# Routed experts as a sparse computation: token rows scattered by expert through DRAM, read back transposed in groups of 384

## The reference, cut to what matters

```
x = x + tanh(g_xattn[0]) * cross_attention(layernorm(x), ctx)
x = x + tanh(g_ffn[0])   * experts(layernorm(x))
x = x + tanh(g_xattn[1]) * causal_attention(layernorm(x), ctx, x)
x = x + tanh(g_ffn[1])   * quantised_linear(layernorm(x))

experts(xt):                                   # xt: 4096 x 256
    scores = sigmoid(xt @ gate_w.T)            # 16 experts
    idx = top_k(scores + gate_b, 4)
    w = scores[idx] / sum(scores[idx]) * 2.5   # four weights of a token
    y = sum over its four experts e of w_e * (silu(xt @ gate_e) * (xt @ up_e)) @ w2_e
    return y + shared_expert(xt)               # one more expert, for every token
```

## Time and profile before

| what | value |
| --- | --- |
| median of 3 runs | 1736.63 us (1736.21 to 1738.77) |
| profiled execution, its own time | 1737.69 us |
| span from the first to the last instruction | 1735.9 us |
| TensorE busy, share of the span | 1439.8 us, 83% |
| VectorE busy | 1275.1 us, 73% |
| ScalarE busy | 636.4 us, 37% |
| GpSimd busy | 326.5 us, 19% |
| mean granted TensorE clock | 0.93 of full speed |

### The profile page before, as it was taken

One profiled execution on the slowest core, in us unless ns is written; L12 is line 12 of the kernel. 1 busy time (PEld: TensorE's weight loads), 2 busy tenths in 40 slices (PEclk: granted clock), 3 DMA queues, 4 the chain that ended last, 5 costly groups with the idle time before them and its releaser, 6 DMA issues. The chain is left out here.

```text
span 1735.9 us, 33621 instructions
## 1 busy us (share of the span) xinstructions
PE 1439.8 (83%) x10080; PEld 756.7 (44%) x10080; DVE 1275.1 (73%) x2834; ACT 636.4 (37%) x936; POOL 326.5 (19%) x340
## 2 busy tenths in 40 slices
PE   4799955999999999999997947887878788888766
PEld 2455532555555555555554522332333233232455
DVE  4999855878787777877667637887878788785475
ACT  0455531111111111111113412665656666666530
POOL 2433332112111121111002050111111111111110
PEclk7999976999999999999998965999999999899998
DMA  5011000000000000000004761111211111110002
GB/s 182 19 37 36 19 1 0 0 0 0 0 0 0 0 0 0 0 0 0 1 0 131 213 170 34 34 34 47 55 35 34 50 51 34 33 34 2 1 0 97
DMA packets 54738, 60.00 MB, mean 35 GB/s; under 512 B 6398, under 2 KB 41982, under 8 KB 54666
## 3 DMA queue, kind: packets, MB, share of 16 engines
q1 hardware_dynamic: 49466, 54.62, 11.1%
q10 hardware_dynamic: 5200, 4.33, 0.8%
HBM read 36.34 MB, written 22.28 MB: 34 GB/s over the span
## 5 line engine op out<-in xcount | busy, mean ns | idle before, releaser
L1461 DVE TENSOR_REDUCE small<-ps 128x1 f32<-128x480 f32 (+6 forms) x768 | 419.2, 596 | 99.7 <-PE ps L1513 91.4
L1439 ACT ACTIVATE region<-ps 128x1024 f32<-128x1024 f32 (+5 forms) x384 | 322.9, 880 | 229.9 <-PE ps L1570 228.2
L956 PE MATMUL ps<-region 128*128 (+1 forms) x1632 | 378.5, 382 | 8.0 <-issue 7.5
L788 ACT ACTIVATE region<-ps 128x512 f32<-128x512 f32 x136 | 81.2, 597 | 446.8 <-PE ps L960 408.8
L956 PEld LDWEIGHTS ps<-region 128*128 (+1 forms) x1632 | 158.9, 98 | 178.4 <-issue 15.9
L1586 PE MATMUL ps<-region 128*32 128x512 f32 (+5 forms) x1792 | 196.7, 512 | 28.3 <-POOL region L1411 21.6
L970 PE MATMUL ps<-region 128*128 (+1 forms) x1632 | 201.7, 273 | 19.6 <-DVE region L896 18.1
L1513 PE MATMUL ps<-region 48*128 48x480 f16 (+6 forms) x896 | 158.7, 344 | 45.6 <-DVE small L1461 44.8
L970 PEld LDWEIGHTS ps<-region 128*128 128x128 f16 x1632 | 156.7, 98 | 63.1 <-DVE region L896 19.4
L1411 POOL TENSOR_SCALAR_AFFINE_SELECT region<-region 128x512 f32<-128x512 f32 (+2 forms) x160 | 87.7, 549 | 491.5 <-ACT region L1439 491.5
L1570 PE MATMUL ps<-region 50*128 50x512 f16 (+5 forms) x896 | 133.7, 334 | 12.7 <-issue 10.5
(11 more groups left out here) (196 smaller groups left out, 1708.6 us busy)
## 6 DMA issues: line engine op xcount, KB each, us to landing
v_parts<-region SPq DMA_DIRECT2D x16, 576.0 KB, 5.8
region<-v_parts SPq DMA_DIRECT2D x16, 576.0 KB, 3.9
region<-k_parts SPq DMA_DIRECT2D x96, 68.0 KB, 2.2
region<-q_parts SPq DMA_DIRECT2D x96, 64.0 KB, 2.1
k_parts<-region SPq DMA_DIRECT2D x16, 272.0 KB, 3.3
x_sb<-in_x ACTq DMA_DIRECT2D x8, 512.0 KB, 9.4
region<-in_w13T SPq DMA_DIRECT2D x16, 256.0 KB, 2.9
q_parts<-region SPq DMA_DIRECT2D x16, 256.0 KB, 3.3
```

Of the source, the lines that this page charges most:

```text
L956: ins = nc.tensor.matmul(o, w(wt, kh, half_), xt[:, kh, cols], start=n == 0, stop=n == 5)
L1439: nc.scalar.activation(dst, src, ACT.Exp, scale=SCALE).then_inc(s_exp, 1)
L1461: nc.vector.tensor_reduce(nmp[:, qt, half, p0:p0 + np_, place], bank[:, 0:np_ * nk].rearrange("p (h k) -> p h k", h=np_), AX.X, ALU.max).t ...
```

## The change: what it does

The expert block is written anew, and the next block gets one more step.

1. **Routing and scatter.** Per chunk, the normalised rows are split into two float16 parts in SBUF (`rows`, 1,044 bytes a token: 1,024 of data, four expert numbers, and the number of the token's first home row). TensorE transposes them, the shared expert is computed on them as before, and the routing runs on four tiles in one instruction where it can (`choose`). The sigmoid comes from ScalarE's tanh. TensorE counts with triangular and all-ones matmuls which place each token has among those of its expert (`ranks`, `slots`). GpSimd then writes each token's row to the four places in a DRAM tensor `xs` that its experts own, by 16 indirect transfers of 128 rows for each chunk.
2. **Tables.** After the last chunk three short TensorE and VectorE steps make tables: which expert group g belongs to and where its rows begin. SyncE writes a fill of 384 spare rows behind each expert's last row.
3. **Groups.** 58 groups of 384 rows, a number that is fixed in the program. SyncE reads a group from DRAM by one transposing transfer into `xgT` and its tags by another transfer. TensorE makes 12 matmuls of 384 columns and 9 of 256; the weights of the expert are addressed through a register. ScalarE makes the silu and the high part, VectorE the product, the low part, the home rows (`homes`) and the copy out of PSUM. GpSimd writes the group's 384 result rows to DRAM (`ys`) by 3 indirect transfers.
4. **Combine.** In the next block, before each chunk's layer norm, GpSimd fetches the four result rows of each of its tokens (2 MB in one transfer, one buffer), and VectorE adds them to x with the token's weights by 16 instructions of 256 columns.

The core of the diff, by engine; its last two parts (`fetch`, `combine`) stand in the next block:

```diff
+GROUP = 3 * P
+GT = GROUP // P
+STRIDE = B * L + GROUP + P
+GROUPS = (B * L * TOPK + E * (GROUP - 1)) // GROUP
+ROW = D + TOPK + 1
+ROW_BUFS = 4
+G_BUFS = 4
+Y_BUFS = 3
+FILLS_AHEAD = 4
...
             @block.sync
+                for b in range(ROW_BUFS):
+                    sp.wait_ge(s_sent[b], CHUNKS // ROW_BUFS * TC * TOPK * 16)
+                sp.wait_ge(s_tabs, 3)
+                def fill_tail(e):
+                    first = sp.value_load(tail_tab[0:1, e:e + 1], min_val=e * STRIDE, max_val=e * STRIDE + B * L)
+                    sp.dma_start(xs[bass.ds(first, GROUP), :].rearrange("(p j) n -> p (j n)", j=GT),
+                                 flat(fill)).then_inc(s_tail[e], 16)
+                for e in range(FILLS_AHEAD):
+                    fill_tail(e)
+                for g in range(GROUPS):
+                    if g + FILLS_AHEAD < E:
+                        fill_tail(g + FILLS_AHEAD)
+                    if g < E:
+                        sp.wait_ge(s_tail[g], 16)
+                    b = g % G_BUFS
+                    if g >= G_BUFS:
+                        sp.wait_ge(s_ggu, g - G_BUFS + 1)
+                        sp.wait_ge(s_home, g - G_BUFS + 1)
+                    first = sp.value_load(start_tab[0:1, g:g + 1], min_val=0, max_val=E * STRIDE)
+                    sp.dma_start_transpose(xgT[:, b].rearrange("p s k n -> p (s k) n"),
+                                           xs[bass.ds(first, GROUP), 0:D].bitcast(F16)).then_inc(s_xg[b], 16)
+                    sp.dma_start(tags[:, b], xs[bass.ds(first, GROUP), D:ROW].rearrange("(j p) n -> p j n", p=P)
+                                 ).then_inc(s_xg[b], 16)
...
             @block.gpsimd
+                for c in range(CHUNKS):
+                    if c + 2 < CHUNKS:
+                        rstd_of(c + 2)
+                    b = c % ROW_BUFS
+                    pool.wait_ge(s_slot, c + 1)
+                    for j in range(TC):
+                        for r in range(TOPK):
+                            at_ = j * TOPK + r
+                            nc.gpsimd.indirect_dma_start(
+                                out=xs, out_offset=bass.IndirectOffsetOnAxis(ap=sloti[:, b, at_:at_ + 1], axis=0),
+                                in_=rows[:, b, j, :], in_offset=None).then_inc(s_sent[b], 16)
+                for g in range(GROUPS):
+                    b = g % Y_BUFS
+                    pool.wait_ge(s_home, g + 1)
+                    pool.wait_ge(s_yout, g + 1)
+                    for j in range(GT):
+                        nc.gpsimd.indirect_dma_start(
+                            out=ys, out_offset=bass.IndirectOffsetOnAxis(ap=home[:, b, j:j + 1], axis=0),
+                            in_=y_out[:, b, j, :], in_offset=None, bounds_check=B * L * TOPK - 1,
+                            oob_is_err=False).then_inc(s_back[b], 16)
...
             @block.vector
+                for c in range(CHUNKS):
+                    choose(c)
+                    if c + 2 < CHUNKS:
+                        statistics(c + 2)
+                    hidden(c)
+                    slots(c)
+                    hidden_low(c)
+                    if c + 2 < CHUNKS:
+                        normalised(c + 2)
+                    add_shared(c)
...
+                for g in range(GROUPS):
+                    if g + 2 < GROUPS:
+                        homes(g + 2)
+                    if g + 1 < GROUPS:
+                        group_hidden(g + 1)
+                    group_out(g)
...
             @block.tensor
+                for c in range(CHUNKS):
+                    shared_gate_up(c)
+                    ranks(c)
+                    if c + 1 < CHUNKS:
+                        transposes(c + 1)
+                        logits(c + 1)
+                    shared_down(c)
...
+                for g in range(GROUPS):
+                    now = ahead
+                    if g + 1 < GROUPS:
+                        ahead = expert(g + 1)
+                        group_gate_up(g + 1, ahead)
+                    group_down(g, now)
...
+                def fetch(c):
+                    pool.wait_ge(s_comb, c * TC * TOPK + 1)
+                    nc.gpsimd.dma_start(yg[:].rearrange("p t r d -> p t (r d)"),
+                                        ys[0:B * L * TOPK, :].rearrange("(c t p r) d -> p (c t) (r d)", p=P, t=TC, r=TOPK)
+                                        [:, bass.ds(c * TC, TC), :]).then_inc(s_yg, 16)
                 for h in range(2):
+                    fetch(h)
                     ln_pool(nc.gpsimd, h, s_var, s_rstd)
                 pool.wait_ge(s_wsplit, 1)
                 with pool.Fori(0, B - 1) as b:
                     context(b)
-                    ln_pool(nc.gpsimd, (b + 1) * 2, s_var, s_rstd)
-                    ln_pool(nc.gpsimd, (b + 1) * 2 + 1, s_var, s_rstd)
+                    for h in range(2):
+                        fetch((b + 1) * 2 + h)
+                        ln_pool(nc.gpsimd, (b + 1) * 2 + h, s_var, s_rstd)
...
+                def combine(c):
+                    dve.wait_ge(s_yg, (c + 1) * 16)
+                    for r in range(TOPK):
+                        for j in range(TC):
+                            n = r * TC + j
+                            if r:
+                                hold(dve, s_comb, c * TC * TOPK + 1 + n - TC + 1, s_tick)
+                            w = weights[:, bass.ds(c * TC + j, 1), r:r + 1].rearrange("p a n -> p (a n)")
+                            nc.vector.scalar_tensor_tensor(out=tile_of(c * TC + j), in0=yg[:, j, r, :], scalar=w,
+                                                           in1=tile_of(c * TC + j), op0=ALU.mult, op1=ALU.add).then_inc(s_comb, 1)
+                    hold(dve, s_comb, (c + 1) * TC * TOPK + 1, s_tick)
                 def normalise(order, b, h):
+                    combine(b * 2 + h)
                     ln_vector(nc.vector, order, b * 2 + h, 1e-5, s_var, s_rstd, s_xn, dst=xn_halves[h])
```

More of the change, by code:

```diff
@@ L941, in comb_transposed @@
[L941 to L952 removed]
+                three = ((0, 0), (1, 0), (0, 1))
@@ new lines, in transposes @@
+                def transposes(c):
+                    if c:
+                        pe.wait_ge(s_xT, 2 * c)
+                    for part in range(2):
+                        pe.wait_ge((s_hi, s_lo)[part], c + 1)
+                        for k in range(KH):
+                            for j in range(TC):
+                                ins = nc.tensor.transpose(xT_ps[part][:, k, j * P:(j + 1) * P],
+                                                          halves(rows, c % ROW_BUFS)[:, j, part, k * P:(k + 1) * P], identh[:])
+                        ins.then_inc(s_xTps, 1)
@@ L953, in gate_up, with logits @@
+                def logits(c):
+                    pe.wait_ge(s_xT, 2 * c + 2)
+                    if c:
+                        pe.wait_ge(s_th, c)
+                    for j in range(TC):
                         n = 0
                         for kh in range(KH):
[L955 to L956 removed]
+                            for part, low in three:
+                                ins = nc.tensor.matmul(lg_ps[:, j * E:(j + 1) * E], xT[:, c % 2, part, kh, j * P:(j + 1) * P],
+                                                       (gwh, gwl)[low][:, kh, :], start=n == 0, stop=n == 5)
@@ new lines, in group_down @@
+                def group_down(g, e):
+                    pe.wait_ge(s_ghl, g + 1)
+                    if g:
+                        pe.wait_ge(s_yout, g)
+                    for j in range(GT):
+                        for n, (part, low) in enumerate(three):
+                            ins = nc.tensor.matmul(ps[:, 6 + j // 2, (j % 2) * D:(j % 2 + 1) * D],
+                                                   (hgh, hgl)[part][:, g % 2, j * P:(j + 1) * P],
+                                                   flat((w2h, w2l)[low][:, bass.ds(e, 1), :]), start=n == 0, stop=n == 2)
+                    ins.then_inc(s_gy, 1)
@@ L1010, in flamingo, with expert @@
+                def expert(g):
+                    return pe.value_load(expert_tab[0:1, g:g + 1], min_val=1, max_val=E)
+                ahead = expert(0)
+                group_gate_up(0, ahead)
+                for g in range(GROUPS):
+                    now = ahead
[3 more added lines that the diff above has]
+                    group_down(g, now)
         reset(region1, region2, small)
```

599 lines of the change are left out of this document (356 added, 243 removed).

## The result

The change makes the kernel slower. Its median is 1883.92 us (1881.56 to 1885.56, 4 runs) against 1736.42 us (1735.32 to 1738.77, 4 runs) for the kernel before on the same chip: a ratio of 1.0846, with a 95% interval of 1.0828 to 1.0865. The prediction was 1662 us, with a range of 1550 to 1830 and a chance of 0.65 for faster. The direction was wrong, and the time lies outside the range.

The account below looks back on a forecast made before the run. TensorE was taken to bound the expert block. Replacing its 668.1 us by 24 + 162 + 12.5 + 295 + 10 = 503.5, plus 90 for the combine, gave about 1662 us; range 1550 to 1830.

Parts of the forecast that it names:

- the period of the groups: Expert block, 58 groups: each takes 4.8 us, the DMA sum, over VectorE 3.7, GpSimd 3.6 and TensorE 3.2.
- The DMA term: Groups: transposing read 2.8 us, tags 0.5, result rows 1.5, together 4.8 us a group.
- Start: Expert block's beginning: layer norm, splitting, logits, choosing, ranks and slots put the first scatter at 24 us.
- scatter: Routing stage: GpSimd's power and 16 indirect transfers at 1.2 us make 20.2 us a chunk, 162 us for eight.
- tables: Between last scatter and first group: landing 3.3 us, four fills, reading the first group; 12.5 us.
- combine: Next block: fetching result rows and adding them, taking turns through one buffer, costs 90 us, bounds 60 to 110.
- The cheap transfers: Scatter and groups: indirect transfers under 1 us, transposing read near 1.4, VectorE sets both stages; 1548 us, chance 0.22.
- The rival of the slower GpSimd: Scatter and groups: GpSimd bounds at 2.0 us an indirect transfer, 33 us a chunk, 6.0 a group; 1834 us, chance 0.15.
- The transposing read in pieces at 62 ns: Groups: the read is paid per 256-byte piece; at 62 ns 8.5 us a group, 1876 us; rival's chance 0.18.
- The nothing-measurable case: Whole kernel: gains of 165 us in the block are returned by combine and scatter; chance 0.03.
- The 0.32 for slower: Whole kernel: the chance of 0.32 that the changed kernel is slower than the one before.
- The locked port: Scatter stage: VectorE's fast SBUF instructions stop GpSimd 1.39 us a chunk, 11 us in all, 1673 us; chance 0.10 within forecast's 0.42.

## Why the prediction was wrong

**The step that failed** is the period of the groups. The prediction took 4.8 us as the largest of the four engines' sums: VectorE 3.7, GpSimd 3.6, DMA 4.8, TensorE 3.2 at full clock. That is right only if enough groups are in flight for each to work on its own. It counted no loop through a buffer. The loop goes from the copy through three transfers of GpSimd, their landing, the wait in `homes` and the products back to the copy. Its pieces were all in the prediction or in its rows, about 0.97 for the copy, 3 x 1.2, a landing of 1.8 to 3.3, and 0.6 + 0.56 + 0.8 + 0.56 on the way back, with one handover to GpSimd. Summed without that handover they are 8.9 to 10.4 us (part of `homes` lies outside the loop, so this is a little high), and measured are 8.42. Had they been added in a row and not set beside each other, the forecast would have been slower. The closing sentence of the prediction names the right place ("a wait of VectorE ... that stands in front of the products, since `homes` for group g + 2 comes before them"), but for the tags' arrival; those were early. The late thing was the reuse of the home buffer, a second wait a few lines further down in `homes`.

**What the runs show of this.** Moving the wait took 4.50 us from each period (8.42 to 3.92), 256 us over 57, and the next block began 255 us earlier (705.0 for 960.0). One more buffer took 3.70. One more transfer added 1.30. All three go as the loop says, the second with 0.5 us less than its 4.21, and none as a rival says.

**The other terms of the groups.** Once the loop is open the period is 3.92 us, near GpSimd's 3 x 1.285 = 3.86, so 4.8 was too high as well. The DMA term was mis-sized: the share of 0.85 is 3.3 us a group, fills included. The plain read leaves 2.3, so the transposing one is about 1.0 over a plain one; with the 1.4 us that the prediction had for the bytes that makes an estimate of 2.4, where it took 2.8 between 1.4 and 4.1. That leaves 0.9 us for tags and result rows, where it took 2.0. No run measures these two by themselves.

**Start, scatter, tables, combine** were right: 24.9 for 24, 172.5 for 162, 13.6 for 12.5, +96.4 for +90. The 1.2 us taken for an indirect transfer, between 0.24 and 2.9 and without a row of its kind, is 0.96 busy and 1.27 from start to start. GpSimd bounds the scatter stage, and one more transfer for each chunk shows it. The order of fetch, combine and power in the next block came as written down, and so did its batch period: 43.4 and 42.0 us from the third combine to the fifth and on to the seventh, for 43.5.

**Two readings that were off** and moved nothing. By the prediction's own pace from the earlier trace rows, 13 x 0.234 + 1.48, the matmuls of an expert are 4.5 us and not 4.3, and 17 of them 77 us, all of the period of 77.8. And the first of the earlier trace rows isn't half clock: twelve in 4.16 us are 1.5 times the full-clock pace and not twice, and the granted clock over this stretch was 0.66. The block was taken out at its measured 668.1 us, and the groups were priced at full clock.

**The rivals.** The cheap transfers failed on both conditions: the step was 1.27 us and not under 1, the read by the estimate above 2.4 and not 1.4; their 1548 us is 82 below even the kernel with the wait moved. The rival of the slower GpSimd, 1834, had the right sign and the wrong cause: GpSimd is busy 44 of 130 us in the groups. The transposing read in pieces at 62 ns had 8.5 us a group and 1876 us, which lie within 1% of the measured 8.42 and 1884, and it was wrong all the same: the reads were early, and with the wait moved the same reads went through in 3.92 us a group. The fit of its numbers is luck. The nothing-measurable case did not come. The 0.32 for slower were spent on prices of engines; no rival was a loop. Of the signs in the profile that the prediction named, the scatter's period (22 for 20 us), the fetches and the next block's length (200.8 for 195) held; "group copies 4.8 us apart" failed, and the first group, 211.0 us after the block's start for 198, came later, mostly by the scatter's 10.5 us.

**The locked port** was put at 11 us, eight times the 1.39 us of four instructions of L210's kind. After the change these are L945, and the trace shows 0.2 us beside them, and a longer delay at another instruction:

```profile
357.66 1.41 DVE L945 TENSOR_SCALAR xn<-x_sb,mv,rstd 128x256 f32<-128x256 f32 x4 [8.37 <-POOL rstd L839]
357.82 1.16 POOL L857 DMA_INDIRECT expert_rows<-region,small  x1 [0.20 <-issue]
...
360.25 1.23 DVE L950 TENSOR_TENSOR region<-xn,region 128x1024 f16<-128x1024 f32 x1 [1.18 <-ACT region L879]
360.55 1.76 POOL L857 DMA_INDIRECT expert_rows<-region,small  x1 [0.30 <-issue]
```

The transfer beside L945 takes 1.16 us in place of 0.96; it is also the first one behind GpSimd's power, so not even these 0.2 us are clearly the port's. In five of the eight chunks one transfer takes 1.70 to 1.77 us. It is the one that starts some 0.3 us into VectorE's subtraction of two SBUF inputs of 1,024 columns (L950), and it ends 0.8 us after that instruction. In the first chunk, where a transfer starts 0.01 us after L950 (272.54 us), it takes 0.96 as the others do. By the group's sums (129.0 us for 128 against 128 x 0.96) all such delays cost 6.1 us. The Trainium skill (SBUF — State Buffer, the two separate sides) says that a GpSimd instruction that reads SBUF and a VectorE instruction with two SBUF inputs exclude each other from the shared port. The trace agrees in kind in these five chunks, by 0.8 us each, and not in the first. That the lock is the cause was not tested by a run.

**Left open.** In the attention behind the next block the kernel with the wait moved is 6 us longer than the changed one (726.7 against 720.5 us, span's end less the first load of queries); the version with two fetches has 720.4 again. TensorE is busy 569.8, 563.2 and 562.3 us in it, at granted clocks of 0.89, 0.91 and 0.91. What sets this clock no run looked into.

## What to carry to other kernels

A pipeline's period is at least the larger of two things: the fullest engine, and for each buffer the time once round (writer, reader, landing, wait, back to the writer) divided by the number of turns that the wait lies behind; write the second sum down for every wait that a change adds. The number of turns is not the number of buffers: it is the number of buffers less how far ahead the waiting instruction runs in its engine's order, here 3 - 2 = 1 (8.42 us) and with four buffers 4 - 2 = 2 (4.21 by the rule, 4.72 measured). Put a wait in front of the instruction that overwrites the large buffer, and give small side data, as these twelve bytes of home rows in each partition, enough buffers that nothing long waits for them.

## What the runs showed of the hardware

- An indirect transfer of 128 rows has a step of 1.27 to 1.29 us on GpSimd, of which 0.96 to 0.98 are busy and 0.30 are a gap, both for rows of 1,044 bytes (L857) and of 1,024 (L865). A GpSimd that is full of them looks a quarter idle: it showed 68.9 of 90 us busy, a share of 0.77, where 70 steps filled the window.
- Such a transfer in the groups lands in a median of 2.4 us from its issue, with 2.0 the shortest. In the loop of the changed kernel the landing took 2.51 of 8.61 us, nearly as much as the 2.57 us between the starts of the first and the third transfer.
- SyncE's transposing read of 393 KB is issued in a median of 1.45 us, where the plain one of the same bytes took 0.39 and the fill of 384 rows (391.5 KB) 0.34.
